# First and fourth attention of a four-layer kernel: halves of queries and keys written straight from PSUM

## The chip, the cores and the metric

The kernel runs on one core of one Trainium2 chip. The metric is the device time of one execution in microseconds (us). TensorE (PE), VectorE (DVE), ScalarE (ACT), GpSimd (POOL) and SyncE (SP) run their own instruction streams and meet at semaphores; SP issues the DMAs that matter here.

## The reference, cut to what matters

Four layers, each an attention and a feed-forward part, on `x` of 16 sequences x 112 tokens x 256 features; the context has 375 tokens. All is fp32. The change touches the attention of the first and the fourth layer, which have 16 heads of width 16:

```python
x = x + _L0_xattn_ref(_layernorm(x), ctx, ctx, ..., mask)        # biases on q, k, v, o
...
x = x + _L3_xattn_ref(_layernorm(x), ctx, ctx, mask, ...)        # no biases

qh = (q @ W_q.T + b_q).reshape(B, S, 16, 16).transpose(0, 2, 1, 3)
kh = (k @ W_k.T + b_k) ...                                        # same shape, 375 keys
scores = einsum('bhqd,bhkd->bhqk', qh, kh) / 4
scores = where(mask == 0, -inf, scores)                           # layer 3: -1e9
attn = softmax(scores); context = einsum('bhqk,bhkd->bhqd', attn, vh)
```

## The kernel before

Both attentions (`ATT[0]` and `ATT[3]`, called first and fourth below) go through one plan, `Att.steps`. A sequence is a batch b; head g = 16 b + h is one step of the plan. At step g all engines work through the same list: PE the scores of head g (L907, into bank g % 2), then the three transposes of the probabilities of head g-3 (L924, "turn"), every fourth step the products with the values (L955), and then what `extras` has put at that step: the projections of the next batch (`gen`): queries q (L830), keys in two parts k0 and k1 (L850), values v (L854), and the late work of the former batch: i (L860, transposed reciprocals), o (L869, the output projection), n and r (L876, L883). DVE takes for each head the masked maximum (L1158, one custom instruction that adds `maskf`, writes `sm` and reduces into `mx`), and copies some of the turned probabilities (L1179); ACT does the exponentials (L1206) and the other copies (L1213). Every engine takes its part of the plan in order. PE may start the scores of head g only when the maximum of head g-2 is done, since they share a bank.

A head has 16 rows, a matmul takes 128. So queries and keys are split in an upper half (rounded to fp32r) and a lower half (the rest), spilled to DRAM (`query_halves`, `key_halves`), and loaded back stacked in `qS` and `kS`, four groups of 32 rows: upper and lower in two combinations, for two neighbouring heads. Of the two heads in a group of 32 rows only one may count in a score, so the queries are written twice, once for even and once for odd heads, with the other head's rows at zero. This is done by DVE at step q: L1065 (first attention, with bias) and L1068 (fourth) multiply the product with `sel2`, which also holds the factor -1/4, into `queries[:, 0]`, 448 wide. ACT writes the keys from PSUM to `keys[:, 0]` (L1236 with bias, L1238 without) and frees the bank. The steps `("split", b, part)` of the plan are DVE's: L1038 casts slot 0 to fp32r in slot 1, L1040 subtracts into slot 2; part 0 are the queries, parts 1 and 2 the keys. In the plan a split stands where the next projection is put, three steps behind its own product.

SP (`stack_sync`) does for each batch in order: spill of the queries (L1279), of k0 (L1282), four loads into `qS` (L1288), four into `kS` (L1292), spill of k1, four more loads, then the context of batch b+2 (L763). The scores of a batch's first head wait for `stacked`, those of its ninth for `stacked8`.

Head numbers in the trace: the scores of head 0 of the first attention start at 49.72 us, those of head 80 at 155.16 us, so the window from 156.5 to 168 us that is used below holds steps 81 to 89: batch 5 is computed, q, k0 and k1 of batch 6 are made at steps 80, 81 and 84, and the norm, i and o of batch 4 stand at steps 84, 85 and 88.

Of the kernel before, what the change touches and what calls it, by code (L numbers as in the profile page):

```python
# [24 lines left out]
F32 = mybir.dt.float32  # L25
# [8 lines left out]
P = 128  # L34
# [76 lines left out]
class Att:  # L111
# [4 lines left out]
    def __init__(self, L, sems, before):  # L116
# [30 lines left out]
        if self.stack:  # L147
            self.spilled = sems[f"spilled{L}"]
            self.split = sems[f"split{L}"]
            self.stacked, self.stacked8 = sems[f"stacked{L}"], sems[f"stacked8{L}"]  # L150
# [30 lines left out]

    def proj(self, b):
# [5 lines left out]
        if self.stack:  # L188
            return q + [(("split", b, 0), 0, 0), k[0], (("split", b, 1), 0, 0), k[1], (("split", b, 2), 0, 0)], v
# [262 lines left out]
def build(nc, A):  # L452
    ctx = ExitStack()
    with ctx:
# [8 lines left out]
        sel16 = sb("sel16", [P, 8])  # L463
# [42 lines left out]
        sel2 = sb("sel2", [P, 2])  # L506
# [3 lines left out]
        keys = wflat[:, 0:6 * SKE].rearrange("p (k o t) -> p k o t", k=3, o=2)  # L510
        queries = wflat[:, 6 * SKE:6 * SKE + 12 * S].rearrange("p (k o t) -> p k o t", k=3, o=2)
        STACK = 32
        NSTACK = P // STACK
        STACK_DMAS = [2 * NSTACK * 16, NSTACK * 16]
# [52 lines left out]
        for L in (0, 3):  # L567
            att_sems[f"spilled{L}"] = [sem(f"l{L}a_spilled{k}") for k in range(3)]
            att_sems[f"stacked8{L}"] = [sem(f"l{L}a_stacked8{k}") for k in range(2)]
            att_sems[f"split{L}"] = sem(f"l{L}a_halves")  # L570
            att_sems[f"stacked{L}"] = [sem(f"l{L}a_stacked{k}") for k in range(2)]
        att_sems["halved"] = sem("l2a_halved")
        folded_ps, folded_sb = sem("l1a_folded_psum"), sem("l1a_folded_sbuf")
# [62 lines left out]
        qhalves = nc.dram_tensor("query_halves", (2, 2 * P, 2 * S), F32).ap()  # L636
# [330 lines left out]
        def att_vector(dve, t):  # L967
            L, H, dh, per = t.L, t.H, t.dh, t.per
            n_chain = t.ch0
            if t.masked:  # L970
# [3 lines left out]
                dve.tensor_scalar(maskf[:, :], m[:, :], 0.0, t.a["fill"], ALU.is_equal, ALU.mult)\  # L974
# [27 lines left out]
            if t.stack:  # L1002
                dve.memset(keys[:, 0, :, SK:SKE], 0.0).then_inc(t.chain, 1)
# [23 lines left out]
            def split(b, part):  # L1027

                a = queries if part == 0 else keys[:, :, part - 1:part, :]
                if part == 0:  # L1030
                    freed(dve, t, t.gen_index("q", b, 0))
                else:
                    freed(dve, t, t.gen_index("k", b, part - 1))
                at = b * 6 + part * 2
                if part and b:
                    former, n = (t.stacked8, STACK_DMAS[1]) if part == 2 else (t.stacked, STACK_DMAS[0])
                    dve.wait_ge(former[(b - 1) % 2], n * ((b - 1) // 2 + 1))
                dve.tensor_copy(a[:, 1].bitcast(F32R), a[:, 0]).then_inc(t.split, 1)  # L1038
                dve.wait_ge(t.split, at + 1)
                dve.tensor_tensor(a[:, 2].bitcast(F32R), a[:, 0], a[:, 1], ALU.subtract).then_inc(t.split, 1)  # L1040

            def gen(kind, b, o, h, n):
# [10 lines left out]
                if kind in "kn" or (kind == "v" and not t.a["bv"]) or (kind == "q" and H == 1):  # L1053
                    return
                dve.wait_ge(t.gen_ready, t.g0 + n + 1)
                if kind == "q" and t.stack:

                    if b:
                        dve.wait_ge(t.stacked[(b - 1) % 2], STACK_DMAS[0] * ((b - 1) // 2 + 1))
                    by_parity = sel2[:, :].unsqueeze(2).broadcast_to([P, 2, S])  # L1060
                    for j in range(t.NO):
                        out = queries[:, 0, j, :].rearrange("p (e s) -> p e s", e=2)
                        q2 = src[:, j * S:(j + 1) * S].unsqueeze(1).broadcast_to([P, 2, S])
                        if t.a["bq"]:
# [1222 lines left out]
```

## Time and profile before

| | us |
|---|---|
| median of 3 runs (lowest, highest) | 2537.48 (2534.27, 2539.64) |
| profiled execution, its own time | 2540.24 |
| its span | 2538.5 |
| PE busy | 2259.6 (89%) |
| DVE busy | 1254.8 (49%) |
| ACT busy | 1046.7 (41%) |

The first attention runs from about 29 to 395 us, the fourth from about 2070 to 2410 us. In section 2 of the page (40 slices of 63.5 us) DVE shows 7 or 8 tenths there and DMA 6 to 8, against 2 to 4 and mostly 0 to 3 in between; PE shows 9 in nearly all slices.

### The profile page before, as it was taken

The page shows a single profiled execution, that of the slowest core. Times are in us where ns is not written, and L with a number is a line of the kernel's source. Part 1 is how long each engine was busy: PE and PEld are TensorE (multiplying, and loading weights), DVE is VectorE, ACT ScalarE, POOL GpSimd, SP SyncE. Part 2 cuts the span into 40 slices and gives each one's busy share as a digit, 9 for nine tenths or more (in the row PEclk, how much of TensorE's full clock was granted, in tenths as well). Part 3 has the DMA queues.
Part 4 walks back from the last instruction along what each step waited for, and adds up shares of the span by engine and source line. Part 5 has one row for each costly group of instructions (what it writes and reads, how often), then busy time and mean ns, then how long its engine had stood idle before and what let it go on. Part 6 is the DMA issues. An engine that isn't in the chain of part 4 may idle for free.

```text
span 2538.5 us, 44680 instructions
## 1 busy us (share of the span) xinstructions
PE 2259.6 (89%) x15374; PEld 1735.6 (68%) x15374; DVE 1254.8 (49%) x3601; ACT 1046.7 (41%) x2814; POOL 294.5 (12%) x342
## 2 busy tenths in 40 slices
PE   4999997999968799859999999999959939999998
PEld 3777775777746667547777777777647727777755
DVE  5787873222243522264444544444542257777712
ACT  2777772222122122124444444444302227778811
POOL 0000001111132145100000000000014400000020
PEclk9999998999979799969999999999969959999999
DMA  6887865222245312310000000000052168888600
GB/s 190 198 199 198 200 165 236 84 83 83 67 127 182 114 52 71 81 50 9 17 7 11 17 7 17 11 10 8 5 194 63 55 174 208 201 197 202 152 11 22
DMA packets 149434, 252.54 MB, mean 99 GB/s; under 512 B 14736, under 2 KB 124640, under 8 KB 146544
## 3 DMA queue, kind: packets, MB, share of 16 engines
q1 hardware_dynamic: 138560, 220.31, 32.3%
q0 software_dynamic: 10656, 29.37, 3.7%
q8 instruction: 131, 2.15, 0.4%
q14 instruction: 87, 0.71, 0.1%
HBM read 191.04 MB, written 58.59 MB: 98 GB/s over the span
## 4 chain that ended last, share of the span: by engine, by line
PE 76%; DVE 12%; issue 4%; DMA 4%; ACT 2%; SPq 0%; POOL 0%; DVEq 0%; ACTq 0%; POOLq 0%
PE bank L1665 8%; PE bank L924 8%; PE bank L955 6%; PE bank L1695 6%; PE bank L839 5%; PE bank L843 5%; PE bank L1720 5%; PE bank L869 4%; PE bank L912 4%; PE bank L854 3%; PE bank L1708 3%; PE bank L830 3%; PE bank L907 3%; PE bank L1992 2%; PE bank L1978 2%
## 5 line engine op out<-in xcount | busy, mean ns | idle before, releaser
L924 PE MATMUL bank<-ident,arena 112*125 112x112 f32 x2352 | 372.0, 276 | 3.4 <-DVE arena L1179 0.3
L924 PEld LDWEIGHTS bank<-ident,arena 112*125 112x125 f32 x2352 | 338.2, 188 | 46.4 <-issue 12.0
L1206 ACT ACTIVATE arena<-arena,mx 112x375 f32<-112x375 f32 x512 | 308.6, 603 | 117.5 <-DVE mx L1158 116.9
L1158 DVE CUSTOM_DVE_ANT_0 arena<-bank,maskf 112x375 f32<-112x375 f32 x512 | 273.6, 543 | 81.8 <-PE bank L907 80.1
L907 PE MATMUL bank<-kS,qS 128*112 128x376 f32 x512 | 235.8, 461 | 47.2 <-DMA kS<-key_halves 23.5
L1170 DVE TENSOR_REDUCE mx<-bank 112x1 f32<-112x375 f32 x256 | 128.9, 543 | 240.1 <-PE bank L912 240.0
L1665 PE MATMUL bank<-arena 128*128 x532 | 229.7, 554 | 3.4 <-ACT arena L1773 2.7
L1179 DVE COPY arena<-bank 125x336 f32<-125x336 f32 x448 | 214.5, 503 | 33.5 <-PE bank L924 33.5
L1206 ACT ACTIVATE arena<-bank,mx 112x375 f32<-112x375 f32 x272 | 156.1, 576 | 171.6 <-DVE mx L1170 150.1
L955 PE MATMUL bank<-arena 125*32 125x112 f32 (+1 forms) x4608 | 202.6, 265 | 2.9 <-DVE arena L1179 2.9
L955 PEld LDWEIGHTS bank<-arena 125*32 125x32 f32 (+1 forms) x4608 | 144.1, 118 | 85.7 <-issue 68.1
L1309 POOL TENSOR_TENSOR rstd<-newton,root 112x2 f32<-112x2 f32 x32 | 22.7, 711 | 1487.7 <-DVE newton L1114 1487.6
L1213 ACT ACTIVATE arena<-bank 125x336 f32<-125x336 f32 x336 | 147.3, 439 | 54.7 <-PE bank L924 51.7
L1695 PE MATMUL bank<-arena 128*128 (+1 forms) x672 | 167.1, 380 | 0.0
L839 PE MATMUL bank<-ctx_halves,weight_halves 128*128 128x376 f32 x768 | 145.5, 342 | 7.6 <-DVE arena L1071 7.6
L843 PE MATMUL bank<-weight_halves,ctx_halves 128*126 128x512 f32 x576 | 148.5, 403 | 0.0
L1720 PE MATMUL bank<-xnT,arena 128*128 128x224 f32 (+1 forms) x640 | 147.4, 376 | 0.3 <-DVEq L647 0.3
L1665 PEld LDWEIGHTS bank<-arena 128*128 128x128 f32 x532 | 99.7, 191 | 65.7 <-issue 47.0
L839 PEld LDWEIGHTS bank<-ctx_halves,weight_halves 128*128 128x128 f32 x768 | 132.1, 191 | 7.8 <-DVE arena L1071 7.8
L907 PEld LDWEIGHTS bank<-kS,qS 128*112 128x112 f32 x512 | 90.8, 178 | 67.8 <-issue 29.8
L1587 POOL DMA_INDIRECT results<-arena,scatter_id x91 | 90.1, 990 | 381.8 <-ACT arena L1795 303.4
L1720 PEld LDWEIGHTS bank<-xnT,arena 128*128 128x128 f32 (+1 forms) x640 | 113.6, 184 | 29.6 <-issue 17.2
(245 smaller groups left out, 3446.7 us busy)
## 6 DMA issues: line engine op xcount, KB each, us to landing
kS<-key_halves SPq DMA_DIRECT2D x256, 188.0 KB, 5.5
qS<-query_halves SPq DMA_DIRECT2D x128, 224.0 KB, 4.6
arena<-in_ctxT SPq DMA_DIRECT2D x64, 376.0 KB, 5.0
key_halves<-arena SPq DMA_DIRECT2D x64, 376.0 KB, 5.2
arena<-in_f_out SPq DMA_DIRECT2D x21, 768.0 KB, 4.6
query_halves<-arena SPq DMA_DIRECT2D x32, 448.0 KB, 4.0
arena<-in_f_up SPq DMA_DIRECT2D x4, 2816.0 KB
arena<-results SPq DMA_DIRECT2D x20, 448.0 KB, 7.7
```

Of the source, the lines that this page charges most:

```text
L839: m = pe.matmul(dst[:, 0:SKE], wH[:, 0, wh, c * t.W + o * P:c * t.W + (o + 1) * P], ctxH[:, ch, c, :], **flags)
L843: m = pe.matmul(dst[0:KT + 1, 0:t.VW], ctxH[:, ch, c, o * KT:(o + 1) * KT + 1], wH[:, 1, wh, c * t.W + h * t.VW:c * t.W + (h + 1) * t.VW], ...
L907: m = pe.matmul(bank[g % 2][0:S, 0:SKE], qS[:, b % 2, h * S:(h + 1) * S].bitcast(F32R), kS[:, b % 2, h // 2 * SKE:(h // 2 + 1) * SKE].bitc ...
L924: m = pe.transpose(bank[2 + g % 2][0:KT, k * S:(k + 1) * S], pr[:, g % t.NR, k * KT:(k + 1) * KT], ident[0:S, 0:S])
L955: m = pe.matmul(out, v, pTv(t, g + j)[:, k, :], **flags)
L1158: dve.tensor_tensor_reduce(sm[:, g % 2, :], bank[g % 2][0:S, 0:SK], maskf[:, :], 1.0, 3e38, ALU.add, ALU.min, mx[:, g % t.NR:g % t.NR + 1])\
L1179: dve.tensor_copy(pTb(t, g), bank[2 + g % 2][0:KT, 0:NKT * S]).then_inc(t.pt_sbuf[1], 1)
L1206: act.activation(pr[:, g % t.NR, :], src, ACT.Exp, bias=mx[:, g % t.NR:g % t.NR + 1], scale=-1.0, accum_out=row_sum(t, b)[:, h:h + 1]).the ...
L1213: act.activation(pTb(t, g), bank[2 + g % 2][0:KT, 0:NKT * S], ACT.Copy).then_inc(t.pt_sbuf[0], 1)
L1665: ins = pe.matmul(bank[m % 2][:, 0:w * f.NU], xTb(n)[:, k, :], up[:, bass.ds(expert[n], 1), at:at + w * f.NU].rearrange("p e n -> p (e n)" ...
L1695: ins = pe.matmul(bank[4 + n % 2][:, 0:D], midT_of(f, m)[:, j * P:(j + 1) * P], w2, start=(q + j == 0), stop=(q == G - 1 and j == J - 1))
L1720: ins = pe.matmul(bank[6][0:w, u * 2 * S:(u + 1) * 2 * S], up[u][:, k, o:o + w], xnT[:, k, c * 2 * S:(c + 1) * 2 * S], start=(u + k == 0), ...
```

## The change

In both attentions, for each batch:

- the queries lose the mask by parity and the factor. `queries` has two slots of 224 columns in place of three of 448; `keys` has two slots in place of three;
- ACT writes the upper half of q, k0 and k1 from PSUM, with the bias, as fp32r (`upper_half`), and raises `upper`. Its key copies stood there before; the query copy is new (two instructions 112 wide in the first, one 224 wide in the fourth attention);
- DVE writes the lower half from the same bank: PSUM (plus bias) minus the upper half (`lower_half`), and it, not ACT, frees the bank. It does so at the step of the product itself and waits there for `upper`. The split steps are gone;
- `qhalves` is half as wide. The loads into `qS` are eight of 16 rows in place of four of 32, and fill only the rows and columns of one parity; the others are zeroed once by POOL at the start of each of the two attentions (`padded`). SP waits for the zeros once, and before a spill for the loads of the batch before;
- the factor goes into the custom instruction of the maximum, and `maskf` is divided by it;
- POOL and DVE no longer make `sel16` and `sel2`.

The core of the diff:

```diff
@@ proj
-        if self.stack:
-            return q + [(("split", b, 0), 0, 0), k[0], (("split", b, 1), 0, 0), k[1], (("split", b, 2), 0, 0)], v
@@ att_vector
+            def lower_half(b, part, src, free):
+                dve.wait_ge(t.upper, t.half_at(b, part))
+                if part == 0 and t.a["bq"]:
+                    for j in range(2):
+                        ins = dve.scalar_tensor_tensor(out=queries[:, 1, j, :].bitcast(F32R), in0=src[:, j * S:(j + 1) * S],
+                                                       scalar=biasA[:, 0, j:j + 1], in1=queries[:, 0, j, :],
+                                                       op0=ALU.add, op1=ALU.subtract)
...
+                elif t.a["bk"]:
+                    ins = dve.scalar_tensor_tensor(out=keys[:, 1, part - 1, 0:SK].bitcast(F32R), in0=src[:, 0:SK],
+                                                   scalar=biasA[:, 1, part - 1:part], in1=keys[:, 0, part - 1, 0:SK],
+                                                   op0=ALU.add, op1=ALU.subtract)
+                else:
+                    ins = dve.tensor_tensor(keys[:, 1, part - 1, 0:SK].bitcast(F32R), src[:, 0:SK],
+                                            keys[:, 0, part - 1, 0:SK], ALU.subtract)
+                ins.then_inc(free, 1)
...
-            def split(b, part):
...
-                dve.tensor_copy(a[:, 1].bitcast(F32R), a[:, 0]).then_inc(t.split, 1)
-                dve.wait_ge(t.split, at + 1)
-                dve.tensor_tensor(a[:, 2].bitcast(F32R), a[:, 0], a[:, 1], ALU.subtract).then_inc(t.split, 1)
...
-                                                 1.0, 3e38, ALU.add, ALU.min, mx[:, g % t.NR:g % t.NR + 1])\
+                                                 -t.a["scale"], 3e38, ALU.add, ALU.min, mx[:, g % t.NR:g % t.NR + 1])\
@@ att_scalar
+            def upper_half(b, part, src):
+                if b:
+                    act.wait_ge(t.spilled[part], t.s0 + 16 * b)
+                if part == 0 and t.a["bq"]:
+                    for j in range(2):
+                        ins = act.activation(queries[:, 0, j, :].bitcast(F32R), src[:, j * S:(j + 1) * S], ACT.Identity,
+                                             bias=biasA[:, 0, j:j + 1])
...
+                ins.then_inc(t.upper, 1)
@@ stack_sync
-                sp.wait_ge(t.split, b * 6 + 2)
-                sp.dma_start(spill(qhalves), queries[:, 1:3]).then_inc(t.spilled[0], 16)
+                if b:
+                    sp.wait_ge(t.stacked[(b - 1) % 2], STACK_DMAS[0] * ((b - 1) // 2 + 1))
+                freed(sp, t, t.gen_index("q", b, 0))
+                sp.dma_start(spill(qhalves), queries[:, :]).then_inc(t.spilled[0], 16)
...
                         for part_ in range(NSTACK):
-                            sp.dma_start(to_q[part_ * STACK:(part_ + 1) * STACK],
-                                         qhalves[part_ // 2].rearrange(pairs, r=STACK)).then_inc(t.stacked[p], 16)
+                            for e in range(2):
+                                row = part_ * STACK + e * 16
+                                sp.dma_start(to_q[row:row + 16, :, e * S:(e + 1) * S],
+                                             qhalves[part_ // 2].rearrange("(g e r) t -> e r g t", e=2, r=16)[e])\
+                                    .then_inc(t.stacked[p], 16)
@@ gpsimd
+            pool.memset(qS[:, :, :], 0.0).then_inc(padded, 1)
```

How this moves instructions. On DVE, in the first attention, from the maximum of head 82 to the reciprocals of batch 4 (steps 82 to 84; L1158 is the maximum, L1179 the copy of turned probabilities, L1038 and L1040 the split of k0; the waits are named), before:

```order
L1158 ISA arena,mx<-bank,maskf 112x375 [waits probs_ready,scores_ready]
L1158 ISA mx 112x1
L1179 COPY arena<-bank 125x336 [waits pv_ready,probsT_in_psum]
L1038 CAST arena<-arena 128x376 [waits l0a_stacked0,product_evacuated0]
L1040 TENSOR_TENSOR arena<-arena 128x376 [waits l0a_halves]
L1135 RECIPROCAL rinv<-sums 112x16 [waits probs_ready]
```

and in the changed kernel, from k0's lower half at step 81 (L1041) on, where L1155 is the maximum and L1176 the copy:

```order
L1041 SCALAR_TENSOR_TENSOR arena<-bank,biasA,arena 128x375 [waits upper_halves,product_ready]
L1155 ISA arena,mx<-bank,maskf 112x375 [waits probs_ready,scores_ready]
L1155 ISA mx 112x1
L1176 COPY arena<-bank 125x336 [waits pv_ready,probsT_in_psum]
L1155 ISA arena,mx<-bank,maskf 112x375 [waits probs_ready,scores_ready]
L1155 ISA mx 112x1
L1155 ISA arena,mx<-bank,maskf 112x375 [waits probs_ready,scores_ready]
L1155 ISA mx 112x1
L1176 COPY arena<-bank 125x336 [waits pv_ready,probsT_in_psum]
L1041 SCALAR_TENSOR_TENSOR arena<-bank,biasA,arena 128x375 [waits upper_halves,product_ready]
L1132 RECIPROCAL rinv<-sums 112x16 [waits probs_ready]
L1135 TENSOR_SCALAR on<-rinv,fac 112x256 [waits attention_chain]
```

The instructions on k0 moved from the end of step 84 to the end of step 81, where k0 is made, and those on k1 from step 87 to the end of step 84, ahead of the reciprocals; both now wait for `upper_halves`.

On PE the order changes at one kind of place, since a split no longer pushes o one step back. After i of a former batch (steps 86 to 88; L907 scores, L924 turn, L869 o), before:

```order
L907 MATMUL bank<-kS,qS 112x376
L924 MATMUL bank<-ident,arena 125x112 x3
L907 MATMUL bank<-kS,qS 112x376
L924 MATMUL bank<-ident,arena 125x112 x3
L907 MATMUL bank<-kS,qS 112x376
L924 MATMUL bank<-ident,arena 125x112 x3
L869 MATMUL bank<-arena,oT 112x256 x2
```

and in the changed kernel (L908 scores, L925 turn, L870 o):

```order
L908 MATMUL bank<-kS,qS 112x376
L925 MATMUL bank<-ident,arena 125x112 x3
L908 MATMUL bank<-kS,qS 112x376
L925 MATMUL bank<-ident,arena 125x112 x3
L870 MATMUL bank<-arena,oT 112x256 x2
L908 MATMUL bank<-kS,qS 112x376
L925 MATMUL bank<-ident,arena 125x112 x3
```

o moved from step 88 to step 87, ahead of the scores of head 88. This happens 14 times in each of the two attentions.

## Rows read from the trace of the kernel before

**Rows 1.** Busy time by stretch: us, then PE, PEld, DVE, ACT, POOL, PEclk, DMA share, GB/s.
```profile
140.00:180.00 40.00, 37.38 (x387) 31.35 (x387) 32.16 (x110) 29.55 (x87) 1.43 (x2) 1.00 0.86 203
2160.00:2200.00 40.00, 37.63 (x386) 31.29 (x384) 30.41 (x105) 31.47 (x94) 1.98 (x2) 1.00 0.83 199
```

**Rows 2.** Waits, 140 to 380 us, last row 2110 to 2390: total, times, longest.
```profile
DVE oT L1049 <- ACT oT L1247: 12.1, 12, 1.0
PE bank L907 <- DVE mx L1158: 9.1, 11, 1.0
...
PE bank L907 <- DVE mx L1158: 11.4, 14, 0.8
```

**Rows 3.** Timeline of PE, steps 81 to 89: start, us, line, operation [idle before].
```profile
158.71 1.51 PE L850 MATMUL bank<-arena 128*128 128x375 f32 x4
...
161.04 0.42 PE L907 MATMUL bank<-kS,qS 128*112 128x376 f32 x1
...
161.94 1.44 PE L850 MATMUL bank<-arena 128*128 128x375 f32 x4
...
164.50 0.41 PE L860 MATMUL bank<-ident,on 112*128 112x112 f32 x2
...
166.71 0.40 PE L907 MATMUL bank<-kS,qS 128*112 128x376 f32 x1 [0.81 <-DVE mx L1158]
...
167.26 1.03 PE L869 MATMUL bank<-arena,oT 128*112 128x256 f32 x4
167.94 0.52 PE L907 MATMUL bank<-kS,qS 128*112 128x376 f32 x1
```

**Rows 4.** Timeline of DVE, same stretch.
```profile
160.43 0.55 DVE L1158 CUSTOM_DVE_ANT_0 arena<-bank,maskf 112x375 f32<-112x375 f32 x1 [0.40 <-PE bank L907]
...
160.90 0.50 DVE L1179 COPY arena<-bank 125x336 f32<-125x336 f32 x1
...
163.88 0.35 DVE L1138 TENSOR_SCALAR on<-rinv,fac 112x256 f32<-112x256 f32 x1
...
165.71 0.39 DVE L1049 TENSOR_TENSOR oT<-bank,oT 128x224 f32<-128x224 f32 x1 [1.01 <-ACT oT L1247]
```

**Rows 5.** Timeline of ACT, same stretch.
```profile
160.26 0.58 ACT L1236 ACTIVATE arena<-bank,biasA 128x375 f32<-128x375 f32 x1 [1.44 <-PE bank L850]
...
163.41 0.57 ACT L1236 ACTIVATE arena<-bank,biasA 128x375 f32<-128x375 f32 x1 [0.18 <-PE bank L850]
...
165.34 0.34 ACT L1247 ACTIVATE oT<-bank 128x224 f32<-128x224 f32 x1
```

**Rows 6.** Groups by shape, 140 to 380 us, last row 2110 to 2390.
```profile
L1077 DVE TENSOR_TENSOR arena<-bank,bvB 125x256 f32<-125x256 f32 x33 | 14.0, 425 | 18.0 <-PE bank L854 17.5
L1040 DVE TENSOR_TENSOR arena<-arena 128x376 fp32r<-128x376 f32 x22 | 12.1, 551 | 0.7
L1040 DVE TENSOR_TENSOR arena<-arena 128x448 fp32r<-128x448 f32 x10 | 6.3, 625 | 0.3
...
L1238 ACT ACTIVATE arena<-bank 128x375 f32<-128x375 f32 x28 | 13.5, 484 | 13.3 <-PE bank L850 13.3
```

**Rows 7.** Timelines of SP and PE at the start of the first attention.
```profile
37.17 0.39 SPq L1279 DMA_DIRECT2D query_halves<-arena  x1
...
39.98 1.82 SPq L1288 DMA_DIRECT2D qS<-query_halves  x4
41.85 1.87 SPq L1292 DMA_DIRECT2D kS<-key_halves  x4
...
49.72 0.66 PE L907 MATMUL bank<-kS,qS 128*112 128x376 f32 x1 [10.76 <-DMA kS<-key_halves]
```

**Rows 8.** PE's timeline: head 16, first attention; heads 0 and 16, fourth.
```profile
69.56 0.43 PE L907 MATMUL bank<-kS,qS 128*112 128x376 f32 x1 [2.39 <-DMA kS<-key_halves]
...
2087.35 0.66 PE L907 MATMUL bank<-kS,qS 128*112 128x376 f32 x1 [8.66 <-DMA kS<-key_halves]
...
2106.56 0.43 PE L907 MATMUL bank<-kS,qS 128*112 128x376 f32 x1 [1.70 <-DMA kS<-key_halves]
```

**Rows 9.** DMA queue, 140 to 380 us: packets, MB, share of 16 engines.
```profile
q1 hardware_dynamic: 37784, 44.14, 76.6%
```

**Rows 10.** POOL's zeroing of the padded values before the fourth attention.
```profile
2057.90 2.66 POOL L2158 MEMSET arena<- 125x3072 f32 x1 [25.72 <-DVEq L647]
```

More of the change, by code:

```diff
@@ L147, in __init__ @@
         if self.stack:
-            self.spilled = sems[f"spilled{L}"]
-            self.split = sems[f"split{L}"]
+            self.spilled, self.upper = sems["spilled"], sems["upper"]
+            self.u0 = 3 * B if L else 0
+            self.s0 = 16 * B if L else 0
             self.stacked, self.stacked8 = sems[f"stacked{L}"], sems[f"stacked8{L}"]
@@ L180, in head, with half_at @@
         return i
+    def half_at(self, b, part):
+        return self.u0 + b * 3 + part + 1
     def proj(self, b):
@@ L567, in build @@
         for L in (0, 3):
-            att_sems[f"spilled{L}"] = [sem(f"l{L}a_spilled{k}") for k in range(3)]
             att_sems[f"stacked8{L}"] = [sem(f"l{L}a_stacked8{k}") for k in range(2)]
-            att_sems[f"split{L}"] = sem(f"l{L}a_halves")
             att_sems[f"stacked{L}"] = [sem(f"l{L}a_stacked{k}") for k in range(2)]
         att_sems["halved"] = sem("l2a_halved")
+        att_sems["spilled"] = [sem(f"halves_spilled{k}") for k in range(3)]
+        att_sems["upper"] = sem("upper_halves")
         folded_ps, folded_sb = sem("l1a_folded_psum"), sem("l1a_folded_sbuf")
@@ L1052, in gen @@
                     return
-                if kind in "kn" or (kind == "v" and not t.a["bv"]) or (kind == "q" and H == 1):
+                if kind == "n" or (kind == "k" and not t.stack) or (kind == "v" and not t.a["bv"]) or (kind == "q" and H == 1):
                     return
                 dve.wait_ge(t.gen_ready, t.g0 + n + 1)
[L1056 to L1064, printed above, removed]
-                            ins = dve.scalar_tensor_tensor(out=out, in0=q2, scalar=biasA[:, 0, j:j + 1],
-                                                           in1=by_parity, op0=ALU.add, op1=ALU.mult)
-                        else:
-                            ins = dve.tensor_tensor(out, q2, by_parity, ALU.mult)
+                if kind in "qk" and t.stack:
+                    lower_half(b, 0 if kind == "q" else 1 + o, src, t.gen_free[n % t.GB])
+                    return
                 elif kind == "q":
@@ L1181, in att_vector @@
                     halve_context(s[1])
-                elif s[0] == "split":
-                    split(s[1], s[2])
                 elif s[0] == "norm":
@@ L1220, in summed_up @@
                     .then_inc(t.norm, 1)
+            def upper_half(b, part, src):
[5 more added lines that the diff above has]
+                                             bias=biasA[:, 0, j:j + 1])
+                elif part == 0:
+                    ins = act.activation(queries[:, 0, :, :].bitcast(F32R),
+                                         src[:, 0:2 * S].rearrange("p (o t) -> p o t", t=S), ACT.Copy)
+                elif t.a["bk"]:
+                    ins = act.activation(keys[:, 0, part - 1, 0:SK].bitcast(F32R), src[:, 0:SK], ACT.Identity,
+                                         bias=biasA[:, 1, part - 1:part])
+                else:
+                    ins = act.activation(keys[:, 0, part - 1, 0:SK].bitcast(F32R), src[:, 0:SK], ACT.Copy)
+                ins.then_inc(t.upper, 1)
             def gen(kind, b, o, h, n):
-                if kind in "or" or (kind == "q" and H > 1) or (kind == "v" and t.a["bv"]):
+                if kind in "or" or (kind == "q" and H > 1 and not t.stack) or (kind == "v" and t.a["bv"]):
                     return
@@ L1226, in gen @@
                 act.wait_ge(t.gen_ready, t.g0 + n + 1)
+                if kind in "qk" and t.stack:
+                    upper_half(b, 0 if kind == "q" else 1 + o, src)
+                    return
                 if kind == "q":
@@ L2176, in _ @@
         def _(act):
-            act.wait_ge(consts, 19)
+            act.wait_ge(consts, 16)
             for L in range(4):
```

65 lines of the change are left out of this document (24 added, 41 removed).

## The prediction

> **What bounds the kernel now.** I read the busy time by stretch first, to see which engine fills the two attentions. PE is busy 37.4 of 40 us in the middle of the first and 37.6 of 40 in the middle of the fourth, at full granted clock; DVE has 32.2 and 30.4, ACT 29.6 and 31.5, and the DMA engines 0.86 and 0.83 of their time [rows 1]. So PE's stream sets the length, and a saving on DVE is worth only what PE waits for DVE. The waits say how much that is: in 240 us of the first attention PE's scores wait 9.1 us for a maximum, 11 times; in 280 us of the fourth 11.4 us, 14 times [rows 2]. That is once a batch, 0.8 us each, and the timeline says where: at head 88 [rows 3], while DVE sits 1.01 us for ACT's copy `oT` [rows 2, 4]. No PE wait in the window stands behind a split. The splits are hidden because they come three steps after their product, when nothing has to be waited for.
>
> **What DVE saves.** Before, a batch costs DVE the masked queries, a cast and a subtraction on 448 columns, and two casts and subtractions on 376 columns; afterwards one short pass over the queries and two subtractions of 375 columns. About 1.9 us per batch go. Since PE hardly waits for DVE's load as such, I count this at nothing by itself. The cover is PE's own work.
>
> **Where the lower halves now stand.** This carries the sum. DVE does k0's lower half at step 81 and cannot go on to the maximum of head 82 before it. I work through one batch of the first attention.
>
> k0: PE's product is complete when ACT starts on it, at 160.26 us [rows 3, 5]. ACT writes the upper half until 160.84. DVE's lower half has 375 columns out of PSUM with a bias; the nearest rows are 551 ns for a subtraction of 376 columns and 425 ns for 256 columns out of PSUM [rows 6]. I take 0.58 us, with 0.5 and 0.65 as bounds, so it ends at about 161.43. Successive instructions overlap by some 0.05 us. The maximum of head 82 then starts at 161.40, not at 160.43 [rows 4]: 0.97 us late. It was already just in time: it ended at 160.98 and PE started the scores of head 84 at 161.04 [rows 3]. These scores therefore start at about 162.05, and k1, behind them in PE's order, about 1.0 us late too.
>
> k1: it starts at 162.9 in place of 161.94 [rows 3], is complete at 164.35, ACT writes its upper half until 164.95, DVE the lower until 165.55. Behind that instruction in DVE's queue stand the reciprocals of batch 4, which took from 163.60 to 164.23 [rows 4]; they now end at 166.15. PE's i needs them. It stood at 164.50 [rows 3] and goes to 166.25: 1.75 us late, of which 1.0 was there. The maximum of head 85 follows on DVE at 166.1, the exponential on ACT, then `oT` at 167.29 in place of 165.34 [rows 5], and DVE's product on `oT` ends at 168.0 where it ended at 166.10 [rows 4].
>
> o: here PE gets something back. Before, it stood idle 0.81 us at head 88 and did o afterwards. Now o is ahead of those scores; it waits until 168.05, fills 0.68 us while DVE does the maximum of head 86, and the scores of head 88 follow at once. Those of head 89 start at about 169.3, against 167.94 [rows 3]. Net **1.33 us per batch** in the first attention. The o move is in this sum; by itself it gives back some 0.5 us.
>
> Behind that point DVE has no split of k1 left and catches up, so nothing further is late. The queries' upper half, new on ACT, takes some 0.6 us (two short instructions; a copy of 224 columns took 0.34) [rows 5], and the maximum of head 81 comes about 0.8 us later than before, but PE asks for it only 1.6 us after its old end, at head 83. I count it at nothing; if that cover were gone, it would cost up to 0.8 us more a batch. ACT has 10 us idle in 40 [rows 1].
>
> The fourth attention has the same steps. ACT's key copy takes 484 ns [rows 6] in place of some 575 [rows 5], and DVE's lower half needs no bias: I take the 551 ns of the row. Two passes, each 0.09 and 0.04 us shorter, make 1.33 - 0.26 = **1.07 us per batch**.
>
> The pattern (k1 ahead of the reciprocals, o one step earlier) occurs 14 times in each: 14 x 1.33 + 14 x 1.07 = **33.6 us** lost. As bounds I take 0.8 and 1.8 us, and 0.6 and 1.5: with 0.5 us less or more at the two waits.
>
> **The DMAs.** Per batch the query spill and the loads into `qS` fall from 448 + 896 KB to 224 + 448 KB; the packets stay 1536, of 448 bytes each. In the middle of a stage the transfers are in time today, so this is worth nothing there. SP has four more issues, 1.82 us for four [rows 7], in a queue that waits for landings anyway. At the start of each attention it counts. In the first, PE waits until 49.72 us [rows 7]. The query spill starts when DVE's lower half of the queries ends, about 35.9 rather than 37.17, and its loads at about 38.6 rather than 39.98. Eight issues end at 42.3, the key loads at 44.1, 0.4 us later than now. Against this stands the volume: 448 KB less, 1.9 us at the 240 GB/s at which the queue runs while busy (44.14 MB in 76.6% of 240 us) [rows 9]. If volume decides, PE starts 3.2 us earlier; if the last issue and a fixed landing time decide, 0.4 later. I take 2.5 us. In the fourth attention, with the same order of issues and 8.66 us of waiting [rows 8], I take 2.3.
>
> The scores of head 16 waited 2.39 and 1.70 us for their loads [rows 8]. In that first batch the lower halves make PE late by about 2 us as well, so the two cover each other: I take a gain of 1 us together. That makes **5.8 us** gained, bounds -1 and 12.
>
> The zeroing of `qS` is 3584 columns; at the pace of 2.66 us for 3072 [rows 10] it takes 3.1 us of POOL, at the start while `x` is still landing, and in the fourth attention until about 2063.7, well before the query spill. It costs nothing. The custom instruction for the maximum keeps its shape.
>
> **Sum.** 33.6 - 5.8 = 27.8 us on the profiled execution's own 2540.24 us: 2568.0. That execution lay 2.76 us above the median of the runs, so I forecast **2565 us**. With the bounds: 14 x (0.8 + 0.6) - 12 = +8, and 14 x (1.8 + 1.5) + 1 = +47.
>
> **Rivals.** (a) The lower halves don't hold PE up. For it: DVE has some 8 us idle in 40 [rows 1]; against it: the idle time lies before products, not after them, and the maximum of head 82 had 0.06 us to spare. Then the o move alone would act: o would start at 166.1 behind the product on `oT`, the scores of head 89 0.6 us earlier, 28 x 0.6 = 17 us, plus 5.8: 2515 us. It decides if head 84's scores still start near 161. Chance 0.08.
>
> (b) The waits are half as long as I think, or the start gains are at their upper bound, and the change comes out level: 2533 to 2542 us. Chance 0.06.
>
> (c) The short packets become the bound. The queue is busy 76.6% of 240 us for 37784 packets, 16 engines: 78 ns a packet on average. If a packet of 448 bytes took 60 ns longer than one of 896 does, a batch would have 1536 x 60 / 16 = 5.8 us more of DMA time on top of the 17 to 18 us that it uses now (0.83 to 0.86 of some 21), more than the 22.4 us that a batch would then last. PE would wait at every batch's first head, 1 us or so, and the starts would be later, not earlier: about 2600 us. Against it: smaller packets should take less, not more. Chance 0.06.
> The Trainium skill ("DMA: Bandwidth & Descriptors", Specifications) states that a transfer below 512 bytes is done by read-modify-write and does not reach line rate. By that rule, the result would be rival (c). No run here shows packets of that size in number, so the trace neither bears it out nor excludes it.
>
> **How the numbers follow.** The forecast, DVE's wait for ACT's upper halves making PE late, has 0.80. The range 2547 to 2583 leaves out (a), (b), (c) and the edges. A measurement of this kernel can tell about 0.2%, 5 us, from no change. Faster by more than that: (a) with a little of (b), 0.09. Within: most of (b), 0.06. Slower: 0.85.
>
> **What would show it.** In the changed profile PE's scores (L908) should wait for the maximum at heads 84, 100, ... by some 0.9 us, i (L861) for DVE's reciprocals by about 0.8, o (L870) for the product on `oT` by about 0.4; DVE's L1041 should wait for ACT in every batch, and DVE be less busy by some 4 us in 40. The first scores should start near 47.2, and the DMA share be below 0.8. I am wrong if the scores of head 84 do not wait, if PE's order after o hides more than 0.5 us, or if loads into `qS` take longer than before.

## The result and the profile after

| | before | after |
|---|---|---|
| median (lowest, highest), us | 2538.48 (2534.27, 2539.64) | 2570.78 (2570.14, 2572.09) |
| span of the profiled execution, us | 2538.5 | 2570.0 |
| PE, DVE, ACT busy, us | 2259.6, 1254.8, 1046.7 | 2258.2, 1200.1, 1059.4 |

The changed kernel is slower: ratio 1.0131, 95% interval 1.0113 to 1.0148. DVE has 55 us less to do, PE as much as before, and the program takes 32 us longer.

The busy time by stretch of the kernel after, with the columns of [rows 1]:

```profile
140.00:180.00 40.00, 34.58 (x348) 28.75 (x347) 27.76 (x97) 27.52 (x82) 1.43 (x2) 1.00 0.62 156
2160.00:2200.00 40.00, 35.47 (x361) 29.11 (x364) 25.70 (x89) 30.07 (x91) 1.99 (x2) 1.00 0.62 160
```

PE is busy 34.6 of 40 us where it was 37.4 [rows 1], at the same full clock; DVE is busy 4.4 us less, and the DMA engines have fallen from 0.86 to 0.62. No engine is full any more: the stage has become a chain of waits. The waits of 140 to 380 us name its links (total, times, longest), to be read against [rows 2]:

```profile
DVE arena L1041 <- ACT arena L1229: 30.9, 22, 1.9
...
DVE arena L1033 <- ACT arena L1223: 15.4, 10, 1.7
...
PE bank L908 <- DVE mx L1155: 9.9, 11, 0.9
PE bank L861 <- DVE on L1135: 9.0, 11, 0.8
...
PE bank L870 <- DVE oT L1056: 5.8, 11, 0.7
```

DVE now stands in front of ACT's upper halves for 46 us in 240, and PE stands three times a batch where it stood once. The timeline of PE over the steps of [rows 3] (head 80 starts at 157.86 here) shows where:

```profile
161.41 1.51 PE L851 MATMUL bank<-arena 128*128 128x375 f32 x4
...
163.17 0.41 PE L908 MATMUL bank<-kS,qS 128*112 128x376 f32 x1
...
164.75 0.43 PE L908 MATMUL bank<-kS,qS 128*112 128x376 f32 x1 [0.86 <-DVE mx L1155]
...
165.65 1.44 PE L851 MATMUL bank<-arena 128*128 128x375 f32 x4
...
169.11 0.38 PE L861 MATMUL bank<-ident,on 112*128 112x112 f32 x2 [0.82 <-DVE on L1135]
...
170.98 1.09 PE L870 MATMUL bank<-arena,oT 128*112 128x256 f32 x4 [0.50 <-DVE oT L1056]
171.72 0.52 PE L908 MATMUL bank<-kS,qS 128*112 128x376 f32 x1
...
172.32 0.40 PE L908 MATMUL bank<-kS,qS 128*112 128x376 f32 x1
```

The first wait is head 84, the second i, the third o; the last two rows are heads 88 and 89. ACT's and DVE's timelines show the hand-over that makes the first two, k0 and then k1. ACT:

```profile
162.95 0.57 ACT L1229 ACTIVATE arena<-bank,biasA 128x375 fp32r<-128x375 f32 x1 [0.65 <-PE bank L851]
...
167.13 0.57 ACT L1229 ACTIVATE arena<-bank,biasA 128x375 fp32r<-128x375 f32 x1 [0.17 <-PE bank L851]
```

and DVE:

```profile
160.52 0.58 DVE L1033 SCALAR_TENSOR_TENSOR arena<-bank,biasA,arena 128x112 fp32r<-128x112 f32 x2 [1.67 <-ACT arena L1223]
...
163.63 0.61 DVE L1041 SCALAR_TENSOR_TENSOR arena<-bank,biasA,arena 128x375 fp32r<-128x375 f32 x1 [1.86 <-ACT arena L1229]
164.15 0.54 DVE L1155 CUSTOM_DVE_ANT_0 arena<-bank,maskf 112x375 f32<-112x375 f32 x1
...
167.80 0.61 DVE L1041 SCALAR_TENSOR_TENSOR arena<-bank,biasA,arena 128x375 fp32r<-128x375 f32 x1 [1.25 <-ACT arena L1229]
168.33 0.24 DVE L1132 RECIPROCAL rinv<-sums 112x16 f32<-112x16 f32 x1
168.61 0.35 DVE L1135 TENSOR_SCALAR on<-rinv,fac 112x256 f32<-112x256 f32 x1
168.88 0.54 DVE L1155 CUSTOM_DVE_ANT_0 arena<-bank,maskf 112x375 f32<-112x375 f32 x1
```

PE's product k0, ACT's 0.57 us, DVE's 0.61 us and the maximum stand one behind the other, and only then may head 84 start. Ahead of the two L1041 DVE stands idle for 1.86 and 1.25 us; the work that it was spared has turned into waiting.

**Where the 31.5 us between the two spans lie.** I took the start of the first scores of each batch in both traces. Head 0 starts 2.0 us earlier than before (47.73, 49.72) and head 16 2.2 us earlier; from there to the end of the first attention 20.6 us are lost. In the stages between the two attentions, which the change doesn't touch, 3.3 us come back (scatter, as shown at the end of the section on the prediction). The fourth attention's head 0 is a further 1.3 us to the good, and 17.7 us are lost after it. -2.2 + 20.6 - 3.3 - 1.3 + 17.7 = 31.5.

### The profile page after: what moved, and what is told of

It reads as the page before. It is cut to its first block, busy times and chain, and to the rows that moved or that the text cites. A ratio compares the mean times of both kernels' runs of the same rounds, so it can differ in the third digit from the quotient of the medians.

```text
span 2570.0 us, 44806 instructions
## 1 busy us (share of the span) xinstructions
PE 2258.2 (88%) x15374; PEld 1731.4 (67%) x15374; DVE 1200.1 (47%) x3456; ACT 1059.4 (41%) x2862; POOL 299.2 (12%) x341
## 4 chain that ended last, share of the span: by engine, by line
PE 76%; DVE 12%; issue 5%; ACT 4%; DMA 2%; SPq 0%; DVEq 0%; POOL 0%; ACTq 0%; POOLq 0%
PE bank L1683 8%; PE bank L925 8%; PE bank L956 6%; PE bank L1713 6%; PE bank L844 5%; PE bank L840 5%; PE bank L1738 5%; PE bank L870 4%; PE bank L913 4%; PE bank L855 3%; PE bank L1726 3%; PE bank L851 3%; PE bank L831 3%; PE bank L908 2%; PE bank L2010 2%
## 5 line engine op out<-in xcount | busy, mean ns | idle before, releaser
L925 PE MATMUL bank<-ident,arena 112*125 112x112 f32 x2352 | 371.0, 275 | 3.3 <-DVE arena L1176 0.3
L925 PEld LDWEIGHTS bank<-ident,arena 112*125 112x125 f32 x2352 | 338.3, 188 | 45.9 <-issue 11.9
L1155 DVE CUSTOM_DVE_ANT_0 arena<-bank,maskf 112x375 f32<-112x375 f32 x512 | 271.0, 542 | 63.5 <-PE bank L908 62.3
L908 PE MATMUL bank<-kS,qS 128*112 128x376 f32 x512 | 236.0, 462 | 44.3 <-DVE mx L1155 26.7
L1176 DVE COPY arena<-bank 125x336 f32<-125x336 f32 x448 | 214.4, 502 | 33.5 <-PE bank L925 33.5
L908 PEld LDWEIGHTS bank<-kS,qS 128*112 128x112 f32 x512 | 91.1, 178 | 65.6 <-DVE mx L1155 31.4
```

The source lines that it names most:

```text
L908: m = pe.matmul(bank[g % 2][0:S, 0:SKE], qS[:, b % 2, h * S:(h + 1) * S].bitcast(F32R), kS[:, b % 2, h // 2 * SKE:(h // 2 + 1) * SKE].bitc ...
L925: m = pe.transpose(bank[2 + g % 2][0:KT, k * S:(k + 1) * S], pr[:, g % t.NR, k * KT:(k + 1) * KT], ident[0:S, 0:S])
L1155: dve.tensor_tensor_reduce(sm[:, g % 2, :], bank[g % 2][0:S, 0:SK], maskf[:, :], -t.a["scale"], 3e38, ALU.add, ALU.min, mx[:, g % t.NR:g % ...
L1176: dve.tensor_copy(pTb(t, g), bank[2 + g % 2][0:KT, 0:NKT * S]).then_inc(t.pt_sbuf[1], 1)
```

## Experiments

Theory (W, for wait): a lower half at the step of its own product makes DVE stand for ACT, and PE for DVE. Rivals: something else in the change costs the time (the smaller packets, more issues on SP, ACT's extra copy, the order of PE), or DVE's saved work is worth something that the waits hide. All experiments are changes to the kernel after or to the one before, and all are compared with the kernel before. In e1 to e5, e8 and e9, `low` steps are put into the plan where the split steps stood.

**All lower halves moved back (e1).**

```diff
@@ proj
+        if self.stack:
+            low = [[(("low", b, part), 0, 0)] for part in range(3)]
+            return q + low[0] + k[0:1] + low[1] + k[1:2] + low[2], v
@@ att_vector, gen
+                if kind in "qk" and t.stack and (0 if kind == "q" else 1 + o) in (0, 1, 2):
+                    return
@@ att_vector, the plan
+                elif s[0] == "low" and s[2] in (0, 1, 2):
...
+                    lower_half(s[1], s[2], bank[t.banks[n % t.GB]], t.gen_free[n % t.GB])
```

> The changed kernel, with the lower halves of queries and keys (DVE's subtraction, with its wait for ACT) put back to the later places at which the splits stood before: q one step after its product, k0 and k1 three steps after theirs; o goes back to its old step (88) too. Everything else of the change stays: ACT's copies, the short packets, the eight loads, the factor in the maximum. Theory W (DVE's in-order wait at the product makes PE late, 1.65 us a batch in the first, 1.26 in the fourth attention): the 38 us are gone, only the earlier start of the two attentions and small things are left, so 2532 to 2538 us, slightly faster than before. Rival A (ACT's new work or its later copies hold the heads up) and rival D (short packets, more issues, or the bank freed later): the loss stays wherever the lower half stands, 2560 to 2571 us.

Measured: 2520.1 us, ratio 0.9922 (0.9899 to 0.9945). With the lower halves at their old places the whole loss is gone, 50 us against the kernel after, although o too is back at its old step, which by itself costs time (e5, e2); but this kernel is also 18 us faster than the one before, which I had not expected. PE's timeline shows the gain at head 88:

```profile
161.65 0.40 PE L911 MATMUL bank<-kS,qS 128*112 128x376 f32 x1 [0.47 <-DVE mx L1162]
```

0.47 us in place of 0.81 [rows 3]. DVE's timelines say why. Before, from the copy of turned probabilities of step 84 to the reciprocals:

```profile
162.34 0.50 DVE L1179 COPY arena<-bank 125x336 f32<-125x336 f32 x1
162.76 0.35 DVE L1038 CAST arena<-arena 128x376 fp32r<-128x376 f32 x1
163.14 0.55 DVE L1040 TENSOR_TENSOR arena<-arena 128x376 fp32r<-128x376 f32 x1
163.60 0.25 DVE L1135 RECIPROCAL rinv<-sums 112x16 f32<-112x16 f32 x1
```

and in e1:

```profile
157.61 0.50 DVE L1183 COPY arena<-bank 125x336 f32<-125x336 f32 x1
158.03 0.60 DVE L1044 SCALAR_TENSOR_TENSOR arena<-bank,biasA,arena 128x375 fp32r<-128x375 f32 x1
158.54 0.24 DVE L1139 RECIPROCAL rinv<-sums 112x16 f32<-112x16 f32 x1
```

From copy to reciprocals 1.26 us became 0.93. Behind the reciprocals come the maximum of head 85, its exponential on ACT, the copy `oT`, the product on it and the maximum of head 86, for which head 88 waits. So the split of k0 stood at the head of that chain all the time, and the view of waits never named it. 28 batches at 0.34 us are 9.5 us of the 18; the other gains are the starts, as in the kernel after, and 3.2 us in the untouched stages, which is within their scatter from one execution to the next.

**The same with o one step earlier (e2).** One more line, so that a `low` step doesn't push o back:

```diff
@@ spread
-                last = slot
+                last = last if step[0] == "low" else slot
```

> As e1_all_late, but o stays at the step where the change put it (87, ahead of the scores of head 88). Theory W: without the lateness of the product on oT, o fills PE's 0.8 us of idle time there: 0.5 to 0.6 us less than e1 for each of 28 batches, 14 to 17 us, so 2517 to 2523 us, faster than both kernels. If o's place is worth nothing: the same as e1.

Measured: 2510.6 us, ratio 0.9883 (0.9858 to 0.9909), 9.5 us better than e1 and the best of all. PE's stream is nearly closed:

```profile
140.00:180.00 40.00, 38.87 (x397) 32.56 (x389) 29.73 (x106) 31.45 (x93) 1.43 (x2) 1.00 0.68 175
```

38.9 us of 40 against 37.4 [rows 1]. It keeps the halves written from PSUM, the unmasked queries through DRAM and the smaller loads, and drops only the places that the changed plan gives to the lower halves. Part of its gain is the place of o and not the code of the halves; e7 below gives that part by itself.

**k0 alone or k1 alone moved back (e3, e4).** As e2, with only part 1 (e3) or only part 2 (e4) late.

```diff
@@ e3, in both places
-                in (0, 1, 2)
+                in (1,)
@@ e4, in both places
-                in (0, 1, 2)
+                in (2,)
```

> The changed kernel, with only k0's lower half three steps later; q's and k1's at their products, o at 87. Theory W, with two waits of their own: the one at head 84 (1.0 us a batch in the first, some 0.85 in the fourth attention) goes, the one at i stays: 14 x 1.85 = 26 us less than the changed kernel, 2545 us. If the two waits were one (what is saved at k0 comes back at k1): 2565 to 2571 us.

> The changed kernel, with only k1's lower half three steps later, behind the reciprocals; q's and k0's at their products, o at 87. Theory W: the wait of i for the reciprocals (0.8 us a batch) and most of what follows at o go, the wait at head 84 stays: 14 x (0.9 + 0.7) = 22 us less, plus up to 5 us at o, so 2543 to 2550 us. If k0's wait alone made the loss: 2565 to 2571 us.

Measured: e3 2545.2 us, ratio 1.0023 (1.0008 to 1.0039), as expected; e4 2535.5 us, ratio 0.9988 (0.9975 to 1.0001), some 10 us better than expected. By batch, from the starts of the first scores in the traces (first attention: batches 2 to 14, counted from 0, since in the kernel before the clock fell in batch 1; fourth: 1 to 14):

| us a batch | before | after | e1 | e2 | e3 (k0 late) | e4 (k1 late) |
|---|---|---|---|---|---|---|
| first | 21.25 | 22.83 | 20.88 | 20.41 | 21.78 | 21.43 |
| fourth | 20.64 | 21.91 | 20.27 | 19.83 | 21.03 | 20.69 |

Against the kernel after, e3 saves 1.05 and 0.88 us, e4 1.40 and 1.22. Their sums, 2.45 and 2.10, are within 0.04 us what e2 saves with all three (2.41 and 2.08). So the two places add up, and the lower half of the queries costs nothing where it stands, though DVE waits 1.67 us there (L1033 in its timeline above). The k1 place is the dearer of the two: it stands at the head of the same chain (reciprocals, maximum of head 85, `oT`), and it is what e3 still has (the waits, 140 to 380 us):

```profile
PE bank L864 <- DVE on L1142: 9.0, 11, 0.8
...
PE bank L873 <- DVE oT L1059: 6.2, 12, 0.7
```

while e4 has only k0's:

```profile
PE bank L911 <- DVE mx L1162: 8.9, 10, 0.9
```

**The o move, from both sides (e5, e7).** e5 is the kernel after with empty `low` steps in the plan, which do nothing but push o back behind head 88. e7 is the kernel before with o at 87:

```diff
@@ e5: att_vector, against e1 in both places
-                in (0, 1, 2)
+                in ()
@@ e7: spread, against the kernel before
-                last = slot
+                last = last if step[0] == "split" else slot
```

> The changed kernel, lower halves at their products, only o back at its old step (88, behind the scores of that head). If the move of o pays also when the product on oT comes late: the scores of head 88 then wait for the maximum of head 86, o comes after, 0.3 us more a batch, 28 batches, 2578 to 2582 us. If it pays nothing there, or costs because PE now stands at o: 2566 to 2572 us.

> The kernel before, splits where they were, only o one step earlier (87). From the 9.5 us between e1_all_late and e2_late_o87, and from 0.81 us of idle time at head 88: 0.4 to 0.6 us less a batch, 2522 to 2529 us. With e2_late_o87 at 2510.6 it also says what the rest of the change is worth once nothing waits at the product: some 14 us. If the o move pays only with the shorter lower half: 2535 to 2540 us.

Measured: e7 2526.5 us, ratio 0.9948 (0.9931 to 0.9964): 12 us, 0.42 a batch, as expected (0.46 by the starts in the traces). What e2 has beyond e7 (2510.6), the rest of the change without its waits, is 16 us; no run divides these among the halves from PSUM, the narrower queries and the smaller loads. e5 2594.8 us, ratio 1.0229 (1.0206 to 1.0252): 24 us more than the kernel after, where I expected 7 to 11. Half of it is the wait. A usual batch takes 23.25 us on average in the first attention and 22.36 in the fourth, 0.44 more than in the kernel after, 12 us in 28. The other half stands in six batches that are some 1.6 us longer than their like. (Inside the two attentions the traces show 22.5 us more; the whole spans differ by 18.4, since the untouched stages ran 3.8 us shorter in e5's execution.) Two batches of the first attention, with the columns of [rows 1], and then a long batch cut finer:

```profile
138.51:163.55 25.04, 21.46 (x198) 17.75 (x199) 16.19 (x59) 16.33 (x49) 0.89 (x2) 0.93 0.57 148
...
186.64:210.14 23.50, 19.91 (x199) 16.42 (x199) 16.18 (x59) 16.32 (x49) 0.91 (x2) 1.00 0.61 158
```

```profile
125.60:127.10 1.50, 0.68 (x6) 0.50 (x5) 0.86 (x4) 0.95 (x4) 0.00 (x0) 1.00 0.97 250
127.10:128.60 1.50, 1.36 (x5) 1.25 (x6) 1.43 (x5) 1.40 (x5) 0.00 (x0) 0.62 1.04 195
128.60:130.10 1.50, 1.50 (x5) 1.07 (x4) 0.00 (x0) 0.93 (x3) 0.00 (x0) 0.50 0.98 282
130.10:131.60 1.50, 1.50 (x29) 1.26 (x27) 1.23 (x4) 0.51 (x2) 0.00 (x0) 0.74 0.18 57
```

The first pair is two batches with the same work, one at 0.93 of the clock and 25.04 us, one at 1.00 and 23.50. The second is from another long batch, the fourth: the granted clock is at 0.50, 1.2 GHz, for 3.4 us from 127.5 on. PE's timeline shows what came ahead:

```profile
120.56 0.42 PE L911 MATMUL bank<-kS,qS 128*112 128x376 f32 x1 [0.86 <-DVE mx L1162]
...
124.91 0.38 PE L864 MATMUL bank<-ident,on 112*128 112x112 f32 x2 [0.82 <-DVE on L1142]
...
127.24 0.42 PE L911 MATMUL bank<-kS,qS 128*112 128x376 f32 x1 [0.96 <-DVE mx L1162]
```

Three waits of under 1 us in 7 us. All six falls of e5 begin at the third wait, from 0.14 us ahead of its end to 0.45 us behind it. But the waits are not enough to tell which batch falls: in the fourth attention, which has three of the six, they are 0.71, 0.67 and 0.96 us, and the other 22 batches have the same waits and no fall, one of them with a third wait of 1.17 us. In the kernel after, where o fills part of the third, no batch from the second on is below 1.00.

**Is it the idle time that costs the clock? (e8, e9)** In e5, PE repeats the scores of head 87 four times (e8) or twice (e9) before it signals them: work without use, which lies just ahead of the third wait.

```diff
@@ att_tensor, scores
+                        for again in range(4 if b and h == 7 else 0):
+                            m = pe.matmul(bank[g % 2][0:S, 0:SKE], qS[:, b % 2, h * S:(h + 1) * S].bitcast(F32R),
+                                          kS[:, b % 2, h // 2 * SKE:(h // 2 + 1) * SKE].bitcast(F32R),
+                                          start=True, stop=True)
```

> The kernel of e5 (o one step back), and PE repeats the scores matmul of head 87 (the eighth head of each batch but the first) four times into the same bank before it signals them: added work that changes no value. It lies just ahead of the 0.96 us for which PE stands at head 88 in e5, so it should fill most of that idle time. In e5's trace six of the 29 full batches are some 1.6 us longer than their like, and show a granted clock of 0.93 in place of 1.00. Theory (the idle time at head 88, third wait in 7 us, is what lets the clock fall): no batch shows 0.93, some 6 x 1.6 = 10 us less than e5, 2582 to 2587 us, although PE does more work. Rival (the falls don't hang on that idle time): the fallen batches stay, 2593 to 2600 us. A repeat that delays the maxima would cost up to 0.3 us a batch more under both.

> As e8, with two repeats of head 87's scores in place of four: idle time at head 88 some 0.65 us in place of 0.96. Theory: fewer fallen batches than in e5, none if the idle time in e5 is only just enough for a fall; 2582 to 2590 us. Rival: 2593 to 2598 us.

Measured: e8 2587.6 us, ratio 1.0197 (1.0171 to 1.0223); e9 2587.3 us, ratio 1.0185 (1.0166 to 1.0204). The third wait shrinks to 0.28 us in e8:

```profile
126.29 0.40 PE L911 MATMUL bank<-kS,qS 128*112 128x376 f32 x1 [0.28 <-DVE mx L1166]
```

and to 0.61 to 0.63 in e9 (in one batch each it is longer, 0.48 and 0.83 us). In both traces all batches but the first of each attention stand at 1.00, and an e8 batch takes 23.41 or 23.09 us, the same as a usual one of e5: the repeats cost nothing, and the falls are gone. Two added repeats do as much as four. By the ratios the gain over e5 is 0.3 to 0.4%, 8 to 11 us, against the 10 that six falls cost; inside the two attentions the traces of e8 and e9 are each 9.7 us shorter than that of e5. Two limits: the intervals of e5 and e8 overlap, and the clock is seen in one execution of each kernel only, while e8's times lie from 2582 to 2595 us, so that a fall may come there as well. That the idle time at head 88 decides in e5 is supported, not closed; e6 below shows that the clock can also fall without that wait. The Trainium skill ("TensorE: Matmul & The Clock Gate", A second HAM failure mode) describes a kernel whose TensorE idles for moments often enough that the clock goes to and fro between its levels; by that rule, e5 is such a case, and its trace agrees in this: the clock falls though no wait ahead of a fall is longer than 0.97 us. That it falls in six batches and not in the other 22 is not explained by the rule, nor by these runs.

**The kernel before with its splits at the product (e6).** The reverse of e1: DVE's cast and subtraction of each half right behind the product, nothing else of the change.

```diff
@@ proj
-            return q + [(("split", b, 0), 0, 0), k[0], (("split", b, 1), 0, 0), k[1], (("split", b, 2), 0, 0)], v
+            return q + k, v
@@ att_vector, the plan
                     gen(*s[1:])
+                    if t.stack and s[1] in ("q", "k"):
+                        split(s[2], 0 if s[1] == "q" else 1 + s[3])
```

> The kernel before (masked queries, ACT's copies, DVE's cast and subtraction in SBUF, long packets, four loads), only with each split at the step of its product; o goes to step 87 by the same rule. Nothing else of the change is in it. Theory W: the in-order wait alone makes the loss, and a little more of it, since cast and subtraction take 0.83 us in place of 0.58: 1.9 to 2.4 us a batch in the first, 1.6 to 2.0 in the fourth attention, no earlier start, 2587 to 2602 us. If the loss comes from ACT's new work, the short packets or the bank's later release: 2525 to 2540 us.

Measured: 2610.4 us, ratio 1.0273 (1.0245 to 1.0301). The place alone, on the old code, makes a slower kernel than the whole change does, a little above what I gave (2602), and the same waits appear (140 to 380 us):

```profile
PE bank L907 <- DVE mx L1160: 12.9, 10, 1.5
PE bank L860 <- DVE on L1138: 10.7, 10, 1.1
```

They are longer than in the kernel after, where one DVE instruction stands in place of these two. The miss above 2602 has the size of a cost that the forecast of this run didn't have: in the profiled execution five batches of the first attention have a granted clock of 0.93 and are 1.6 to 1.9 us longer than their like, 8 us together. One of them and one of its like, with the columns of [rows 1]:

```profile
166.45:191.19 24.74, 21.86 (x205) 18.09 (x204) 16.54 (x54) 15.27 (x45) 0.53 (x1) 0.93 0.69 166
214.95:238.10 23.15, 20.26 (x205) 16.84 (x204) 16.37 (x54) 15.34 (x45) 0.50 (x1) 1.00 0.75 178
```

PE stands before o here for only 0.5 us; the waits at head 84 and at i are 1.13 to 1.46 and 1.0 to 1.1 us, and one of the five falls comes right behind the wait at head 84. The batches without a fall take 23.45 us in the first attention and 22.75 in the fourth, 2.2 and 2.1 more than before: the first inside, the second just above what I gave. The difference between e6 and the kernel after, 40 us by the medians and 36 by the spans of the two traces, is thus not the price of one thing. Of the 36, 21 us lie in the usual batches (0.65 and 0.84 us each, where e6 keeps all of the old work and of the old loads), 8 in the clock, 5 in the starts and first batches and 1.5 in the stages between. e1 and e6 together settle the cause: the step at which the halves are made decides, in both codes.

## Why the prediction was right, point by point

Forecast 2565 us, measured 2570.8, inside the range; the likeliest case was the one that came. That it came within 6 us is partly luck: the loss in the attentions was taken 4.7 us too small and the gains at the starts 2.4 us too large, and 3.3 us of scatter in untouched stages hid part of both. The terms:

| term | predicted, us | measured, us |
|---|---|---|
| k0's lower half, delay of head 84 | 1.0 a batch | 1.01 (head 83 to 84: 1.58 for 0.57) |
| k1's lower half, further delay of i | 0.75 | 0.90 (k1 to i: 3.46 for 2.56) |
| from i to head 89, given back | 0.42 | 0.23 (3.21 for 3.44) |
| net a batch, in steps 83 to 89 | 1.33 | 1.68 |
| both attentions, 28 batches | 33.6 | 38.3 |
| start of the first attention | -2.5 | -2.0 |
| start of the fourth | -2.3 | -1.3 |
| head 16, both | -1.0 | -0.1 (-0.2 and +0.1) |
| stages between | 0 | -3.3 |

The 38.3 us are less than 28 times the 1.68 of one stretch. Over a whole usual batch the loss is 1.58 us in the first attention and 1.27 in the fourth (1.07 was taken there). And the first attention's second batch loses only 0.1 us: the kernel before has a clock fall there, 3.4 us at 0.50 from 71.2 us on, behind its 2.39 us wait at head 16, and the kernel after has neither that wait nor the fall.

- **What bounds it.** PE sets the length: e2 fills PE to 38.9 of 40 and is the fastest. But the step "No PE wait in the window stands behind a split", and with it "I count this at nothing by itself" for DVE's saved work, failed: e1 shows 0.34 us a batch. I had looked at the wait's own releaser only, the maximum of head 86, and not followed the chain back through ACT. In the kernel after the gain doesn't show, because k1's lower half has come into the same chain in k0's place.
- **k0.** Right in mechanism and size: the lower half took 0.61 us (0.58 taken), ACT's upper half 0.57, and the maximum had no slack. e3 prices the place at 1.05 and 0.88 us. (The first list of DVE's order in the section on the change begins at the maximum of head 84, not of head 82; those of 82 and 83 stand ahead of it, at 160.43 and 161.32 us.)
- **k1.** Right in mechanism, a bit too small. DVE takes it up 0.10 us after ACT's end and needs 0.03 us more than taken. e4 prices the place at 1.40 and 1.22.
- **The o move.** "By itself some 0.5 us": e5 and e7 show 0.44 and 0.42. What is given back from i to head 89 was taken too high, 0.42 for 0.23: from i to o it is 1.87 us (1.80 taken), from o to head 88 0.74 (0.68), and head 89 follows 0.60 us later. That in e5 the clock falls once o is moved back was not in the prediction, and costs nearly as much again.
- **The queries.** Counted at nothing; e2 to e4 add up without them.
- **The starts.** Right in sign, 3.4 us for 5.8. SP's timeline at the first start, with the columns of [rows 7]:

```profile
35.64 0.39 SPq L1290 DMA_DIRECT2D query_halves<-arena  x1
...
37.96 3.65 SPq L1305 DMA_DIRECT2D qS<-query_halves  x8
41.66 1.85 SPq L1310 DMA_DIRECT2D kS<-key_halves  x4
```

The spill goes out 1.5 us earlier than in [rows 7] and its loads 2.0 us earlier, and the eight issues take 1.8 us more than the four, so the key loads are issued at 41.66 for 41.85: 0.2 us are left. From the end of these issues to head 0 it is 4.2 us (43.51 to 47.73) where it was 6.0 (43.72 to 49.72): 1.8 us, near the 1.9 that the prediction worked out for the smaller volume (no run changes the volume alone). What failed is the 0.5 us on top, and head 16: it waits for no load any more, and the time comes back as waits for a maximum in the first batch, 1.58 us at head 5 and 0.99 at head 8 (0.70 and 0.83 in the fourth attention). The prediction had this cover and let 1 us of gain through; only 0.1 is left.
- **Rival (c), the short packets.** It fell. The queue's row for 140 to 380 us:

```profile
q1 hardware_dynamic: 37333, 35.46, 57.9%
```

Against [rows 9] this is nearly the same number of packets with 20% fewer bytes in 24% less time: 60 ns a packet on average for 78. By size, the same stretch of the two traces has 16896 packets of 896 bytes at 61 ns on average before, and 16386 of 448 bytes at 29 ns after. The Trainium skill's rule ("DMA: Bandwidth & Descriptors", Specifications) has transfers below 512 bytes done by read-modify-write and off the line rate. The trace doesn't bear out that they cost more time here, neither each nor per byte: half the bytes took half the time.
- **The stages between.** The 3.3 us are no effect of the change. From the last scores of the first attention to the first of the fourth it is 1705.0 us before and 1700.4 after (1.3 of the difference is the start). In the traces of the nine experiments the same stretch takes from 1696.6 (e5) to 1708.4 us (e2), with a mean granted clock from 0.937 to 0.928; e7, which changes nothing but o's place, has 1703.9. So such differences come and go from one execution to the next, with the clock.
- **What stays open.** Why the clock falls in some batches and not in others with the same waits, and how the 16 us of e2 over e7 divide among the parts of the change.

## What to carry to other kernels

Moving a step to "where its input is made" saves its work and turns distance into waiting: in an engine that takes its list in order, everything behind the step waits too, and here the places of two steps of 0.61 us cost 2.4 us a batch in the first attention. Before such a move, write down for each engine what stands behind the step and how much slack its last reader has; and where a wait bounds a kernel, follow it back through all engines before counting a saved instruction at nothing, since the view of waits names only the last link. Take the cheaper code and keep the old place: that was e1, 0.8% faster than before, and with o one step earlier e2, 1.2% faster, where the change as made was 1.3% slower.

## What the runs showed of the hardware

- The granted clock of TensorE fell to 0.50 for 3.4 us at a time though no wait ahead of it was longer than 1.5 us. In e5 it fell in six of 28 batches, behind waits of 0.86 to 0.91, 0.82 and 0.96 us in the first attention and 0.71, 0.67 and 0.96 in the fourth; with the third wait at 0.6 or 0.3 us, in one batch of each kernel longer, no such batch of the profiled execution fell (e9, e8). In e6 it fell in five: in four behind waits of 1.13 to 1.46, 1.08 and 0.5 us, in one right behind the first of them (1.45). Batches with the same waits and no fall are more frequent in both. A short wait can thus cost more than its length: some 1.6 us for each fall.
- Loads into `qS` of 56 KB in 448-byte packets land 2.3 us after their issue (median of 256, section 6 of the page); the loads of 224 KB in 896-byte packets did so in 4.6 us (median of 128).
- ACT and DVE read one bank after each other, DVE 0.10 us behind ACT's end. ACT's instruction takes 571 ns on average in 140 to 380 us, with fp32r output, for 574 before with fp32. DVE's takes 607 with a bias, and 549 without one in the fourth attention (2110 to 2390 us).
- Packets of 448 bytes took 29 ns of a DMA engine's time on average (kernel after, 140 to 380 us), those of 896 bytes 61 ns (kernel before).
